# Chunk 3's second score block in the scan banks: a pair of PSUM banks per wide score, as the plan names it

## The reference

```python
h = rmsnorm(x, ln1_w)
q = (h @ wq).reshape(b, s, H, HD)          # 16 heads of 128
k = (h @ wk).reshape(b, s, H, HD)
v = (h @ wv).reshape(b, s, H, HD)
scores = jnp.einsum('bqhd,bkhd->bhqk', q, k) / np.sqrt(HD).astype(np.float32)
scores = jnp.where(causal, scores, jnp.float32(-1000000000.0))
attn = jax.nn.softmax(scores, axis=-1)
ao = jnp.einsum('bhqk,bkhd->bqhd', attn, v).reshape(b, s, H * HD) @ wo
x = x + ao
```

## Time and profile before

| | us |
|---|---|
| median of 3 runs | 1388.28 (1384.49 to 1389.0) |
| the profiled execution | 1393.36, of which its span 1391.7 |
| busy over the span: PE / weight loads / DVE / ACT / POOL | 1118.5 / 868.5 / 1040.8 / 597.1 / 579.8 |

### The profile page before, as it was taken

One profiled execution on the slowest core, in us unless ns is written; L12 is line 12 of the kernel. 1 busy time (PEld: TensorE's weight loads), 2 busy tenths in 40 slices (PEclk: granted clock), 3 DMA queues, 4 the chain that ended last, 5 costly groups with the idle time before them and its releaser, 6 DMA issues. The chain is left out here.

```text
span 1391.7 us, 16990 instructions
## 1 busy us (share of the span) xinstructions
PE 1118.5 (80%) x5224; PEld 868.5 (62%) x5224; DVE 1040.8 (75%) x1899; ACT 597.1 (43%) x1539; POOL 579.8 (42%) x471
## 2 busy tenths in 40 slices
PE   4657345597696889968967999899989989999797
PEld 2335223475585677746746876687858857676586
DVE  5978999899898999898988965999743433343433
ACT  5534545455663336455743323666431123333210
POOL 2646566753565777645866710577200000000000
PEclk9978779799798999998989999999999999999899
DMA  3473134343254866334756621456325532331163
GB/s 132 140 264 107 52 112 137 94 139 103 87 171 150 260 179 192 116 98 125 216 177 190 207 89 65 141 193 216 113 80 164 161 124 86 102 102 57 57 197 110
DMA packets 105434, 191.54 MB, mean 138 GB/s; under 512 B 11648, under 2 KB 42368, under 8 KB 105088
## 3 DMA queue, kind: packets, MB, share of 16 engines
q1 hardware_dynamic: 91520, 177.42, 40.1%
q10 hardware_dynamic: 13824, 13.05, 2.9%
HBM read 176.33 MB, written 14.09 MB: 137 GB/s over the span
## 5 line engine op out<-in xcount | busy, mean ns | idle before, releaser
L1925 DVE TENSOR_TENSOR_SCAN scan_banks<-scan_banks,h_end,drive 128x256 f32<-128x256 f32 x512 | 360.2, 747 | 2.1 <-ACT scan_banks L1663 1.3
L2278 POOL TENSOR_TENSOR sum<-sum,state 128x512 f32<-128x512 f32 x174 | 226.6, 1302 | 93.3 <-DVE state L1935 92.2
L2257 POOL TENSOR_TENSOR drive<-w1T,bc_rows 128x512 f32<-128x512 f32 x128 | 163.5, 1279 | 148.2 <-DVE scan_banks L1925 67.1
L2257 POOL TENSOR_TENSOR drive<-w0T,bc_rows 128x512 f32<-128x512 f32 x128 | 164.1, 1283 | 125.8 <-DVE scan_banks L1925 71.2
L1935 DVE TENSOR_TENSOR state<-scan_banks,bc_rows 128x512 f32<-128x512 f32 x256 | 174.7, 683 | 0.3 <-issue 0.2
L2281 POOL TENSOR_TENSOR stats_b<-stats_b,neg_half 128x2 f32<-128x2 f32 x12 | 8.3, 693 | 393.3 <-DVE stats_b L2095 213.2
L1534 PE MATMUL score_banks<-kv,qT 128*128 128x512 f32 (+3 forms) x384 | 150.4, 508 | 26.7 <-ACT probs L1825 23.1
L2110 DVE TENSOR_REDUCE soft<-score_banks 128x1 f32<-128x128 f32 (+7 forms) x128 | 95.6, 751 | 97.4 <-PE score_banks L1536 96.6
L1559 PE MATMUL work_bank<-probsT,kv 128*128 128x256 f32 (+1 forms) x588 | 141.4, 364 | 4.7 <-ACT probsT L1836 2.7
L1384 PE MATMUL score_banks<-state,ident 128*128 128x256 f32 x256 | 77.6, 431 | 78.9 <-DVE state L1935 78.9
L1825 ACT ACTIVATE probs<-score_banks,soft 128x128 f32<-128x128 f32 (+7 forms) x128 | 94.4, 739 | 77.8 <-DVE soft L2110 76.4
(11 more groups left out here) (203 smaller groups left out, 1976.6 us busy)
## 6 DMA issues: line engine op xcount, KB each, us to landing
bc_rows<-bc_rows SPq DMA_DIRECT2D x256, 256.0 KB, 3.4
streamed_w<-in_w_head SPq DMA_DIRECT2D x64, 384.0 KB, 4.9
expert_w<-in_w_moe SPq DMA_DIRECT2D x52, 384.0 KB, 4.4
kv_past<-kv ACTq DMA_DIRECT2D x48, 256.0 KB, 3.7
kv<-in_w_moe SPq DMA_DIRECT2D x32, 384.0 KB, 4.1
kv<-kv_past SPq DMA_DIRECT2D x16, 768.0 KB, 4.7
kv<-kv_past SPq DMA_DIRECT2D x16, 512.0 KB, 5.1
streamed_w<-in_w_moe SPq DMA_DIRECT2D x16, 384.0 KB, 4.2
```

The source lines that it names most:

```text
L1925: done = e.engine.tensor_tensor_scan(states, states, drive[g % len(drive)][:, i, 0:size], h_end[layer][:, n, kt:kt + 1], ALU.mult, ALU.add)
L2257: self.tt(drive[g % len(drive)][:, :, 0:size], w_of(layer, c)[:, PAIR * half:PAIR * (half + 1), 0:size], rows_of(g, c, 0), ALU.mult).then_ ...
L2278: self.tt(to, so_far, slot_of(c, layer, k), ALU.add).then_inc(added, 1)
```

## The change

A score of more than 512 keys is written to, and read from, the pair of banks that the plan recorded for it: the pair 0 and 1 (`score_banks`), or the pair 5 and 6 (the first two of `scan_banks`). Before, it always lay in the pair 0 and 1, whatever the plan had booked.

```diff
         def score_bank(c, h, qb):
 
+            i = plan.bank["score", c, h, qb]
             if keys(c, qb) > BANK:
-                return (0, 1), score_banks
-            i = plan.bank["score", c, h, qb]
+                return (i, i + 1), scan_banks[:, 0:2 * BANK] if i else score_banks
             return (i,), shared[i]
```

## The result

The changed kernel takes 1364.22 us (median of 4 runs, 1359.42 to 1364.86) against 1386.54 us (4 runs, 1384.49 to 1389.0) of the kernel before on the same chip: a ratio of 0.9831 with a 95% interval of 0.98 to 0.9861. The two medians lie 22.3 us apart; by the ratio it is 23.4 us.

What follows compares the result with a forecast made beforehand. PE's queue was taken to bound chunk 3's heads, idling 19.5 us for exponentials of earlier scores. Gains of 4.0 + 7.3 + 15.1 = 26.4 us off the median 1388.28 us gave 1362 us, range 1357 to 1370.

Steps and rivals of the forecast that it cites:

- What bounds the stage: Last third, chunk 3: PE's queue sets the time; its score matmuls wait 19.5 us, 16 times, for an earlier score's exponential.
- Heads 4 to 15, 12 x 1.26 = 15.1 us: Chunk 3: block 1's scores start 1.18 us sooner and take 0.10 us less per head; low bound 12.1 us.
- The slack stays 0.28 us: At the next head's turn: block 1's exponential still ends 0.28 us ahead, since the whole chain moves forward by 1.26 us.
- Heads 2 and 3, 7.3 us: Chunk 3: three PE waits in a row, 5.04 us, shrink to some 0.25 us; 7.3 us gained, 5.0 if the clock falls.
- The other 2.2 us are the clock: Heads 2 and 3: beyond 5.04 us of waits, 2.2 us of gain comes from full clock instead of 0.56.
- Head 1, 4.0 us: Chunk 3: without the 2.35 us wait and slow scores, the router starts at 1028.86, not 1032.90; low bound 2.5 us.
- Sum: Whole kernel: 26.4 us gained, bounds 19.6 and 28, taken off the median 1388.28 to give 1362 us.
- A: Rival: freed time partly returns at the next turn, 0.6 us per head; gain 19 us, 1369 us; 12 in 100.
- B: Rival: maximum and exponential read banks 5 and 6 slower while PE writes others; 1400 us at 2.25 times; 3 in 100.
- C: Rival: the wait was not PE's limit, or moved scores wait for former bank users; within 4 us of 1388.28; 3 in 100.
- D: Rival: granted clock falls in heads 4 to 15 after the change, costing 26.4 us; 1388 us; 1 in 100.

Runs made afterwards that it cites:

- two kernels with a late maximum: Changed kernel plus an unused DVE maximum ahead of block 1's in heads 4 to 15: over 64 keys 1361.09 us, over 1024 keys 1370.34 us.
- the kernel with heads 4 to 15 alone: Against the kernel before, only block 1 of heads 4 to 15 of chunk 3 moves to banks 5 and 6: 1374.68 us, ratio 0.9885.
- the run with block 0's waits: Changed kernel, but block 0 of each head of chunk 3 after head 0 waits again for the preceding block's exponential: 1368.1 us in one run.

## Why the prediction was right

1362 us with a range of 1357 to 1370 was forecast; 1364.22 and 1364.6 were measured. By its own steps:

- *What bounds the stage.* Right: PE's idle was the kernel's time. In heads 4 to 15 it was taken away and came back in full in the span.
- *Heads 4 to 15, 12 x 1.26 = 15.1 us.* Right: 15.27 in the profile, 16.0 (12.5 to 19.3 by its interval) by itself. The period fell to 11.71 or 11.72, as forecast (11.73). Both parts of the 1.26 are there: the scores start 1.17 us sooner behind the apply and take 0.10 less.
- *The slack stays 0.28 us.* Right: 0.29. The two kernels with a late maximum show that the number was one to stand on. 0.15 us more costs nothing in these heads, 1.14 us more costs 0.95 where the turn is tight. The prediction counts the tight turn in all twelve heads; it is in ten of them, and head 15's chain ends in the wait of 0.49 us.
- *Heads 2 and 3, 7.3 us.* The three waits went as walked through (the turn of head 2 waits a little, as forecast: it starts 0.29 us behind the start of the mask's matmul ahead of it, where 0.06 is usual), and against that one execution it is 7.16. As a price for the kernel **this term was mis-sized**: "The other 2.2 us are the clock" was taken from an execution in which the clock fell fully, and in two of four traces of the kernel before it did not fall. There the gain is 14.7 - 9.0 = 5.7 us, and over the four traces 15.2 - 9.0 = 6.2 us. So even in the first trace the clock made 16.19 - 14.71 = 1.5 us of the 7.3 and not 2.2; of the other 0.7, 0.2 is that the wait ahead of head 3's block 0 was 1.51 us there and is 1.73 us behind fast scores, and the rest is what the stops cost beyond their idle at full clock. Over the four traces the clock is worth 0.5 us here. So not all that a slow clock costs is lost: DVE and ACT go on while PE works slowly, and PE stands less ahead of head 3's block 0 (1.51 and 0.83 us behind slow scores).
- *Head 1, 4.0 us.* Right as a sum, 4.06, and its clock is slow in most executions. Where it is not (the kernel with heads 4 to 15 alone, 7.59 us from block 0 to the router, against 9.08 - 4.06 = 5.02) the step gives 2.6 us.
- *Not foreseen*: 1.67 us between the router and head 2. The four traces of the kernel before take 88.53, 89.24, 86.93 and 88.64 us there, 88.3 in the mean, against 86.86 and 86.85 in the two of the changed kernel: 1.5 us. Slow experts make it in two, the slow projections ahead of them in one, and in one nothing does. Two of the four also have a stop of PE of 0.44 or 0.59 us for a transfer (`streamed_w`), which the run with block 0's waits has too (0.59), so that part is not the change's.
- *Sum.* 4.0 + 7.3 + 15.1 = 26.4 was forecast against one execution and taken off the median. With 6.2 for heads 2 and 3 it is 25.3, and with 1.5 for the stretch between the router and head 2 it is 26.8. The measured 22.3 and 25.3 us have intervals that overlap (19.3 to 27.7 and 22.1 to 28.5), so they don't tell these sums apart.
- *Rivals.* A: no wait at the next turn, and the run that made one shows what it costs. B: maximum and exponential are as long as before. C: the list of waits is empty of it. D: the clock is 1.00 over the 143.87 us, before the change as after it. The rule of the Trainium skill, "TensorE: Matmul & The Clock Gate", section "A second HAM failure mode: psum-queue depth-cycling", foresees a clock that goes up and down where PE cycles through PSUM banks with short stops; neither kernel's trace shows that in these heads, with stops of 1.01 us twelve times or with none.

What stays open is why the same stop of 2.3 us lets the clock fall in one execution and not in the next, and why the experts' clock was full in all seven traces of kernels without head 1's stop (or with it filled) but one. No experiment here moves that by itself. The Trainium skill, "TensorE: Matmul & The Clock Gate", section "What's actually happening", says that the clock's supervision runs free of the program, so that the moment of a change of clock varies from run to run. The traces agree in so far as the same 2.31 us stop was followed by scores of 1.98, 2.50 and 3.41 us; that this is the cause, no run here shows.

No run points to a version that beats the changed kernel: PE has no idle left in these heads, and the waits that remain (4.5 us for the normalised tokens, 2.5 us in the experts) are not for banks.

## What to carry to other kernels

Where a wait for a buffer stands on the bounding engine, price it by the distance between starts, not by the idle shown: here 1.01 us of idle was worth 1.26 us a head, and the same holds for the new wait (0.73 shown, 0.95 paid). Then find the next instruction that needs the same producer, and count the slack there; 0.28 us was enough here, because the whole chain moved with the score. A term that rests on a slow clock in one profiled execution is a term with a chance on it: profile several executions of the unchanged kernel before you book it.

## What the runs showed of the hardware

- Behind the same stop of PE of 2.31 us the same scores took 1.98, 2.50 or 3.41 us. The fall can set in at once, part of the way through, or not at all; behind the stop at head 1 it was seen in five of six traces, behind that at head 2 in two of six, and behind one of 2.30 us in the experts in five of twelve.
- The clock did not always come back soon: in the fourth trace of the kernel before the granted clock was 0.50 from 1030.36 to 1039.30 us, 8.9 us long, while PE stood still for only 0.93 us of it. From the mask of head 1's block 0 to the experts' matmuls it was 16.20 us, against 14.20 us in the trace of heads 4 to 15 alone, with full clock behind the same stop: the fall cost 2.0 us, since it also filled the wait of 2.30 us for DVE.
- A stop costs more than its idle, at full clock too: the scores behind a stop took 1.98 us against 1.88 without one, and the overlap of about 0.17 us with the group ahead is lost. The 1.98 us came behind stops of 0.54, 1.01, 1.22 and 2.31 us alike.
- Maxima and exponentials of 1024 keys took 1.23 and 1.11 us from the scan banks while PE wrote into other banks, and 1.22 and 1.12 us from the score banks.
- A maximum over 64 keys took 0.23 us by its row but held up the next instruction by only 0.15 us.
